# A top-6 expert layer on one core: routed rows scattered plainly to a place per token, weighted and summed at the end

## The chip, the cores and the metric

The kernel runs on one core of a Trainium2 chip. The metric is the device time of one execution in microseconds. The core has five engines that run their own instruction streams and meet at semaphores: PE (matmul), DVE (vector), ACT (scalar, activations), POOL (GpSimd) and SP (which only issues DMAs here). Sixteen DMA engines move data for them.

## The reference

`x` is [2, 512, 256], so T = 1024 tokens of H = 256. `xn = layernorm(x)`, and the output is `x + attention(xn) + moe(xn)`.

```
q, k, v = xn @ Wq + bq, xn @ Wk + bk, xn @ Wv + bv        # 8 heads of 32
# decayed linear attention, head h with factor g[h], per sequence of 512:
out[i] = sum over j <= i of g**(i-j) * (q[i].k[j]) * v[j]   # done in chunks, with a carried state

scores = softmax(xn @ gate_w.T)                            # 64 experts
topk_w, topk_ids = top_k(scores, 6);  topk_w /= sum(topk_w) + 1e-20
routed = sum over the 6 experts e of a token:
           topk_w * (silu(xn @ Wg[e]) * (xn @ Wu[e])) @ Wd[e]   # inner width 176
shared = (silu(xn @ SG) * (xn @ SU)) @ SD                  # inner width 352
moe = routed + shared
```

## The kernel before, in words

The kernel is written engine by engine; each engine's block is its program in order, and every dependency is a semaphore wait.

**Routing.** `x` is loaded as 8 chunks of 128 tokens, normalised on DVE into `tab`, and written by POOL to the HBM tensor `table` (1024 rows: 256 values of the token and 64 weights, one per expert, zero where the expert wasn't chosen). PE makes the logits, DVE finds the top six (`chosen`), PE counts ranks, and one-hot matmuls turn them into lists of up to 128 tokens per expert, a column of `gidx` each (gather indices; padding points beyond the table and is skipped) and of `sidx` (scatter indices; padding points to spare rows behind the 1024). POOL computes the normalised weights. Q, K and V are made on PE in the same stage. POOL also zeroes two accumulators `acc[0]` and `acc[1]` of 1152 rows in HBM.

**Experts.** 66 tiles follow: one for each of 64 experts and two extra ones (`EXTRA`) for experts with more than 128 tokens (a loop behind them for still more isn't entered with these inputs). Tile t, with k its place in a ring of 16: SP loads the weights (480 and 48 KB) into a slot of the ring up to 16 tiles ahead. POOL gathers the tile's rows (`gather`, L423) 8 tiles ahead with the index column `gcol`. PE transposes them (L1090), ACT and DVE split them and the weights in a high and a low part (L547, L775; L541 and `w_low`, L770), PE multiplies (L1104, six matmuls), ACT applies silu (L553), DVE multiplies gate, up and the token's weight (`gate_up`, L762), PE transposes (L1114) and multiplies by the down weights (L1132, L1133), ACT copies the result from PSUM to `y` (`evac_y`, L566; four buffers), and POOL adds the 128 rows to `acc[k % 2]` (`scatter`, L429, an indirect DMA that accumulates). Two scatters into one accumulator must not be under way together, so `store` waits for the one two tiles earlier:

```
pool.wait_ge(acc_done[k % 2], (t - k) * 8 + 16 * (k // 2 + 1))
pool.sem_inc(pool_waited, 1)
scatter(k)
```

POOL's order is: gather for tile t + 8, scatter of tile t - 1, and so on. DVE writes the columns `scol` (L858) and `gcol` (L863) at the end of each tile's work. The lists of the two extra tiles are made during the last tiles; their gathers come `LATE` = 4 places later than the rhythm, directly ahead of the scatters of tiles 59 and 60.

**Shared expert and attention.** PE multiplies six blocks (L1202) with DVE's product (`sprod`, L940, in the buffer of `y`, so the first one waits for all scatters) and ACT's silu; between them DVE adds biases to K and V, scales K (`ks`) and Q (`qsT`) and copies `kT`. Then 8 chunks of 128 tokens: scores on PE (`scores`, L1213), the product by `decay` on DVE (L968), the shared expert's down matmuls (L1236), the state's matmul and its update on DVE (L987; L991 and L992 from the second chunk of a sequence on; none in the fourth), the output matmuls (L1256) into the same PSUM bank, and DVE's final addition into `res` (L978, L997), which SP stores. What it adds was loaded from the two accumulators (1 MB each) and summed with `x_again` by POOL, 16 additions (L499, L502).

## Time and profile before

| | |
|---|---|
| time, median of 3 runs | 343.68 us (342.89 to 348.36) |
| profiled execution, its own time | 344.82 us |
| its span, first to last instruction | 343.0 us |
| mean granted TensorE clock | 0.943 of full speed |
| PE / DVE / ACT / POOL busy | 297.7 / 189.1 / 152.0 / 225.6 us |
| DMA moved | 64.88 MB |
| first expert matmul (L1104) | 50.57 us |
| last expert matmul (L1133) ends | 279.9 us |

Busy time is the union of an engine's instructions; waits and semaphore handling aren't in it. The difference between the profiled execution's time and its span, 1.8 us, lies before the first and behind the last instruction.

### The profile page before, as it was taken

Reading aid. Unit: us, or ns where it says so; the run is one execution under the profiler, and the core shown is the slowest. Engines: PE = TensorE matmul, PEld = TensorE weight load, DVE = VectorE, ACT = ScalarE, POOL = GpSimd, SP = SyncE. Lnnn points to the kernel's source line nnn. Section 1 sums busy time; section 2 is a strip of 40 time slices with the busy share of each in tenths; the row PEclk is TensorE's granted clock in tenths of the full one; section 3 lists DMA queues with packets and bytes.
Section 4 is the critical chain, followed back from the end, with each engine's and each line's share of the span. In section 5 each row is a group of like instructions: output and inputs, shape, how many; then the busy total and the mean of one; then the engine's idle time right before and its main releaser. Section 6 shows DMA issues by size and latency. Waiting matters only on the chain.

```text
span 343.0 us, 6367 instructions
## 1 busy us (share of the span) xinstructions
PE 297.7 (87%) x1608; PEld 211.0 (62%) x1608; DVE 189.1 (55%) x541; ACT 152.0 (44%) x400; POOL 225.6 (66%) x176
## 2 busy tenths in 40 slices
PE   8938888998798778979798988899883999989996
PEld 7814766775476655646465665677562643549996
DVE  4587758863544444535455454548762245845553
ACT  1635356665554646455555556465661232230000
POOL 1566547877787778878888788888865555359200
PEclk9996999999879899999999999969998589999999
DMA  7999619999989798999889999877962436300000
GB/s 204 361 396 341 188 43 309 274 268 264 247 209 241 174 286 210 232 245 235 235 228 241 239 223 256 234 160 174 208 122 35 46 35 145 129 0 32 32 32 32
DMA packets 34870, 64.88 MB, mean 189 GB/s; under 512 B 5451, under 2 KB 23063, under 8 KB 34848
## 3 DMA queue, kind: packets, MB, share of 16 engines
q1 hardware_dynamic: 21216, 44.42, 41.0%
q0 software_dynamic: 13632, 20.20, 29.7%
q8 instruction: 10, 0.16, 0.2%
q14 instruction: 12, 0.10, 0.1%
HBM read 54.17 MB, written 13.37 MB: 197 GB/s over the span
## 4 chain that ended last, share of the span: by engine, by line
DMA 31%; PE 28%; issue 17%; DVE 10%; POOL 10%; ACT 2%; POOLq 1%; SPq 0%; DVEq 0%; ACTq 0%
DMA acc<-y,scol 28%; PE ps L1104 6%; POOL acc L429 6%; POOL digits L423 4%; PE ps L1256 3%; PE ps L1202 3%; PE ps L1133 3%; PE ps L1236 2%; PE ps L1132 2%; DVE one_hots L715 2%; PE ps L1213 2%; DMA digits<-table,gcol 2%; PE ps L1090 1%; DMA x_slab<-in_x 1%; DVE neg_max L694 1%
## 5 line engine op out<-in xcount | busy, mean ns | idle before, releaser
L429 POOL DMA_INDIRECT acc<-y,scol x66 | 105.7, 1602 | 36.0 <-issue 16.7
L1104 PE MATMUL ps<-w_split,xT_both 128*128 128x352 f32 x396 | 92.6, 362 | 25.0 <-ACT xT_both L547 24.4
L1104 PEld LDWEIGHTS ps<-w_split,xT_both 128*128 128x128 f32 x396 | 64.8, 198 | 57.9 <-ACT w_split L541 30.1
L423 POOL DMA_INDIRECT digits<-table,gcol x66 | 76.4, 1158 | 23.4 <-issue 15.2
L762 DVE SCALAR_TENSOR_TENSOR act<-ps,digits,sg 128x176 f32<-128x176 f32 x64 | 25.6, 400 | 93.0 <-ACT sg L553 91.0
L566 ACT COPY y<-ps 128x256 f32<-128x256 f32 x66 | 24.7, 374 | 94.4 <-DMA acc<-y,scol 78.8
L770 DVE TENSOR_TENSOR w_split<-w_ring,w_split 128x704 fp32r<-128x704 f32 x66 | 58.3, 884 | 1.1 <-PE ps L1104 0.3
L541 ACT CAST w_split<-w_ring 128x704 fp32r<-128x704 f32 x66 | 51.7, 784 | 0.0
L1133 PE MATMUL ps<-w_slab,aT 48*128 48x256 f32 x132 | 48.5, 449 | 0.0
L1132 PE MATMUL ps<-w_ring,aT 128*128 128x256 f32 x132 | 43.2, 412 | 0.0
L1133 PEld LDWEIGHTS ps<-w_slab,aT 48*128 48x128 f32 x132 | 20.6, 196 | 24.2 <-issue 24.2
L1090 PE MATMUL ps<-k,digits 128*128 128x128 f32 x132 | 26.8, 286 | 6.6 <-DMA digits<-table,gcol 6.6
L775 DVE TENSOR_TENSOR xT_both<-ps,xT_both 128x256 fp32r<-128x256 f32 x66 | 27.4, 415 | 6.9 <-ACT xT_both L547 6.8
L1114 PE MATMUL ps<-k,act 128*128 128x128 f32 x132 | 27.2, 291 | 0.0
L547 ACT CAST xT_both<-ps 128x256 fp32r<-128x256 f32 x66 | 24.6, 373 | 5.6 <-PE ps L1090 5.3
L559 ACT COPY aT<-ps 128x256 f32<-128x256 f32 x66 | 25.6, 388 | 0.4
L553 ACT ACTIVATE sg<-ps 128x176 f32<-128x176 f32 x66 | 21.1, 320 | 8.8 <-PE ps L1104 7.8
L1090 PEld LDWEIGHTS ps<-k,digits 128*128 128x128 f32 x132 | 19.2, 147 | 8.9 <-DMA digits<-table,gcol 6.1
L1132 PEld LDWEIGHTS ps<-w_ring,aT 128*128 128x128 f32 x132 | 21.9, 208 | 0.3 <-issue 0.3
L1202 PE MATMUL ps<-xnT,sgu_sb 128*128 128x512 f32 (+1 forms) x48 | 21.4, 595 | 0.6 <-ACT y L566 0.6
L1114 PEld LDWEIGHTS ps<-k,act 128*128 128x128 f32 x132 | 17.9, 150 | 0.5 <-issue 0.5
L491 POOL TENSOR_TENSOR sact_lo<-y,sact_hi 128x512 fp32r<-128x512 f32 (+1 forms) x6 | 8.4, 1412 | 12.4 <-ACT sact_hi L631 12.4
(161 smaller groups left out, 356.1 us busy)
## 6 DMA issues: line engine op xcount, KB each, us to landing
w_ring<-in_w SPq DMA_DIRECT2D x66, 480.0 KB, 3.7
w_slab<-in_w SPq DMA_DIRECT2D x66, 48.0 KB, 4.4
acc<-zero POOLq DMA_DIRECT2D x2, 1152.0 KB, 16.5
routed_sums<-acc SPq DMA_DIRECT2D x2, 1024.0 KB, 7.0
digits<-table,gcol POOLq DMA_INDIRECT x66, 4.2
acc<-y,scol POOLq DMA_INDIRECT x66, 5.2
x_slab<-in_x SPq DMA_DIRECT2D x4, 256.0 KB, 3.4
table<-tab_slab POOLq DMA_DIRECT2D x1, 1024.0 KB, 9.1
```

Source lines behind the costliest of these rows:

```text
L423: pool.indirect_dma_start(out=rows[:, r, :], out_offset=None, in_=table, in_offset=bass.IndirectOffsetOnAxis(ap=gcol[:, r:r + 1], axis=0), ...
L429: pool.indirect_dma_start(out=acc[k % 2], out_offset=bass.IndirectOffsetOnAxis(ap=scol[:, k % 8:k % 8 + 1], axis=0), in_=y[:, k % 4, :], i ...
L541: nc.scalar.copy(rr(w_hi[:, k % 4, :]), w1_sb[:, k % RING, 0:4 * F]).then_inc(whi_sb, 1)
L559: nc.scalar.copy(aT[:, k % 2, :], ps[4 + k % 2][:, 0:2 * P]).then_inc(aT_sb, 1)
L770: V.tensor_tensor(rr(w_lo[:, k % 2, :]), w1_sb[:, k % RING, 0:4 * F], w_hi[:, k % 4, :], ALU.subtract).then_inc(wlo_sb, 1)
L775: V.tensor_tensor(rr(xT_lo[:, k % 2, :]), ps[k % 2][:, 0:H], xT[:, k % 2, :], ALU.subtract)\
L1090: ins = nc.tensor.transpose(ps[k % 2][:, h * P:(h + 1) * P], rows[:, r, h * P:(h + 1) * P], ident)
L1104: ins = mm(ps[2 + k % 2][:, 0:2 * F], rr(a[:, k % 2, h * P:(h + 1) * P]), rr(b[:, k % (2 if b is w_lo else 4), h * 2 * F:(h + 1) * 2 * F]) ...
L1114: ins = nc.tensor.transpose(ps[4 + k % 2][:, h * P:(h + 1) * P], act[:, k % 2, h * P:(h + 1) * P], ident)
L1132: mm(ps[6 + k % 2][:, 0:H], aT[:, k % 2, 0:P], w1_sb[:, slot, 4 * F:W1C], start=True, stop=False)
L1133: mm(ps[6 + k % 2][:, 0:H], aT[0:F2, k % 2, P:2 * P], w2_sb[0:F2, slot, :], start=False, stop=True).then_inc(y_ps, 1)
L1202: ins = mm(ps[(m % 2) * 2 + o][0:fw, :], sgu_sb[:, k, o * FS + f * P:o * FS + f * P + fw], xnT[:, k, n * 512:(n + 1) * 512], start=(k == 0 ...
```

## The change

Nothing is accumulated in HBM any more. Each token gets six rows of a new HBM tensor `parts` (6144 rows of 256), one for each expert it chose. The row's number for token and expert is found by a running count over `chosen` (`dest`), and it takes the place of the weight in the table's last 64 columns, so that it comes with the gathered row. `scol` is made from it; padding points beyond `parts` and is skipped. DVE's product in `gate_up` no longer has the token's weight. `store` waits only for `y` and `scol`; the four buffers of `y` have a semaphore each (`y_out`), for which ACT's copy waits four tiles later. After the experts SP loads `parts` chunk by chunk ([128, 6, 256], three buffers), ACT scales each of the six rows by its weight (`part_w`, which DVE makes in the shared expert's stage with six pairs of a product and a reduction over the 512 columns), and DVE reduces the six to one and adds `x_again`, into which it has put the PSUM result. POOL's 16 additions, the zeroing and the two loads of 1 MB go.

```diff
-    acc = [nc.dram_tensor(f"acc{k}", [ACC_ROWS, H], f32, kind="Internal").ap() for k in range(2)]
+    parts = nc.dram_tensor("parts", [T * TOPK, H], f32, kind="Internal").ap()
...
-            for k in range(2):
-                sp.dma_start(acc_sb[k], acc_v[k][:, 0:NC, :]).then_inc(acc_in, 16)
-            for c in range(NC):
-                sp.wait_ge(res_sb, c + 1)
-                sp.dma_start(out_v[:, c, :], res[:, c % 2, :]).then_inc(out_done[c % 2], 16)
+            for c in range(NC + PART_BUFS):
+                if c >= PART_BUFS:
+                    done = c - PART_BUFS
+                    sp.wait_ge(res_sb, done + 1)
+                    sp.dma_start(out_v[:, done, :], res[:, done % 2, :]).then_inc(out_done[done % 2], 16)
+                if c < NC:
+                    if c >= PART_BUFS:
+                        sp.wait_ge(parts_read, c - PART_BUFS + 1)
+                    b = c % PART_BUFS
+                    sp.dma_start(part_sb[b], parts_v[:, c, :, :]).then_inc(parts_in[b], 16)
...
-            for k in range(2):
-                pool.dma_start(acc_v[k], zero[:].unsqueeze(1).to_broadcast([P, ACC_ROWS // P, H]))\
-                    .then_inc(acc_done[k], 16)
...
+            pool.wait_ge(dest_ready, 1)
+            pool.dma_start(table_v[:, :, H:ROW], dest.rearrange("p (c e) -> p c e", e=E)).then_inc(table_out, 16)
             pool.wait_ge(share_ready, 1)
...
             def scatter(k):
                 pool.indirect_dma_start(
-                    out=acc[k % 2], out_offset=bass.IndirectOffsetOnAxis(ap=scol[:, k % 8:k % 8 + 1], axis=0),
-                    in_=y[:, k % 4, :], in_offset=None, compute_op=ALU.add).then_inc(acc_done[k % 2], 16)
+                    out=parts, out_offset=bass.IndirectOffsetOnAxis(ap=scol[:, k % 8:k % 8 + 1], axis=0),
+                    in_=y[:, k % Y_BUFS, :], in_offset=None, bounds_check=T * TOPK - 1,
+                    oob_is_err=False).then_inc(y_out[k % Y_BUFS], 16)
...
                 pool.wait_ge(scol_ready, t + 1)
-
-                pool.wait_ge(acc_done[k % 2], (t - k) * 8 + 16 * (k // 2 + 1))
                 pool.sem_inc(pool_waited, 1)
                 scatter(k)
...
-            for c in range(NC):
-                G.tensor_tensor(acc_sb[1][:, c, :], acc_sb[1][:, c, :], acc_sb[0][:, c, :], ALU.add)\
-                    .then_inc(pool_step, 1)
-                pool.wait_ge(pool_step, c + 1)
-                G.tensor_tensor(acc_sb[1][:, c, :], acc_sb[1][:, c, :], x_again[:, c, :], ALU.add)\
-                    .then_inc(xab_ready, 1)
...
-                    act_e.wait_ge(acc_done[k % 2], (t - k) * 8 + 16 * (k // 2))
-                nc.scalar.copy(y[:, k % 4, :], ps[6 + k % 2][:, 0:H]).then_inc(y_sb, 1)
+                    act_e.wait_ge(y_out[k % Y_BUFS], (t - k) * (16 // Y_BUFS) + 16 * (k // Y_BUFS))
+                nc.scalar.copy(y[:, k % Y_BUFS, :], ps[6 + k % 2][:, 0:H]).then_inc(y_sb, 1)
...
             high_product(5)
+            act_e.wait_ge(part_w_ready, TOPK)
+            for c in range(NC):
+                act_e.wait_ge(parts_in[c % PART_BUFS], 16 * (c // PART_BUFS + 1))
+                for k in range(TOPK):
+                    ins = nc.scalar.activation(part_sb[c % PART_BUFS][:, k, :], part_sb[c % PART_BUFS][:, k, :],
+                                               ACT.Identity, scale=part_w[:, c, k:k + 1])
+                ins.then_inc(parts_scaled, 1)
...
             dve.wait_ge(chosen_ready, 1)
+            dve.wait_ge(ex_ready, NC)
+            dve.wait_ge(c32_in, 16)
+            flat = chosen[:].rearrange("p c e -> p (c e)")
+            V.tensor_tensor_scan(dest[:], flat, flat, c_32("dest_first"), ALU.add, ALU.max).then_inc(dest_ready, 1)
...
-                V.tensor_copy(scol[:, k % 8:k % 8 + 1], sidx[:, bass.ds(t, 1)]).then_inc(scol_ready, 1)
+                    V.scalar_tensor_tensor(scol[:, k % 8:k % 8 + 1], rows[:, k % AHEAD, bass.ds(t + H, 1)], -1.0,
+                                           pad[:, bass.ds(t, 1)], ALU.add, ALU.add).then_inc(scol_ready, 1)
...
+            def part_weights(k):
+
+                if k > 0:
+                    dve.wait_ge(part_w_ready, k)
+                V.scalar_tensor_tensor(ov_sel[:], dest.rearrange("p (c e) -> p c e", e=E), float(k), exm[:],
+                                       ALU.is_equal, ALU.mult).then_inc(dve_step, 1)
+                step[0] += 1
+                dve.wait_ge(dve_step, step[0])
+                V.tensor_reduce(part_w[:, :, k], ov_sel[:], AX, ALU.add).then_inc(part_w_ready, 1)
...
+                if n == 0:
+                    dve.wait_ge(comb_ready, 1)
+                    V.tensor_tensor(dest.rearrange("p (c e) -> p c e", e=E), dest.rearrange("p (c e) -> p c e", e=E),
+                                    bc(c_32("dest_base"), [P, NC, E]), ALU.subtract).then_inc(rel_ready, 1)
+                    dve.wait_ge(rel_ready, 1)
+                part_weights(n)
...
+            def finish(c):
+                dve.wait_ge(o_ps, 2 * (c + 1))
+                if c == 0:
+                    dve.wait_ge(x_again_in, 32)
+                V.tensor_tensor(x_again[:, c, :], ps[4 + c % 2][:, 0:H], x_again[:, c, :], ALU.add)\
+                    .then_inc(o_sb, 1)
+
+            def sum_parts(c):
+                dve.wait_ge(parts_scaled, c + 1)
+                V.tensor_reduce(total[:, c % 2, :],
+                                part_sb[c % PART_BUFS].rearrange("p k h -> p h k"), AX, ALU.add).then_inc(parts_read, 1)
+                dve.wait_ge(parts_read, c + 1)
+                dve.wait_ge(o_sb, c + 1)
+                if c >= 2:
+                    dve.wait_ge(out_done[c % 2], 16 * (c // 2))
+                V.tensor_tensor(res[:, c % 2, :], x_again[:, c, :], total[:, c % 2, :], ALU.add).then_inc(res_sb, 1)
...
                 if c >= 1:
-                    finish = c - 1
-                    dve.wait_ge(xab_ready, finish + 1)
...
+                    finish(c - 1)
                 m = c % SEQ_CHUNKS
                 if m == SEQ_CHUNKS - 1:
+                    sum_parts(c - 1)
                     continue
...
+                if c >= 1:
+                    sum_parts(c - 1)
+            finish(NC - 1)
+            sum_parts(NC - 1)
```

The extra tiles get their destinations from the gathered rows too, with two small operations each (`extra_dest`) that were made for the weight before.

## Rows read from the trace of the kernel before

**Rows 1.** The page's chain that ended last, by engine and line.

```profile
DMA acc<-y,scol 28%; PE ps L1104 6%; POOL acc L429 6%; POOL digits L423 4%; PE ps L1256 3%; PE ps L1202 3%; PE ps L1133 3%; PE ps L1236 2%; PE ps L1132 2%; DVE one_hots L715 2%; PE ps L1213 2%; DMA digits<-table,gcol 2%; PE ps L1090 1%; DMA x_slab<-in_x 1%; DVE neg_max L694 1%
```

**Rows 2.** Waits from 66 to 270 us: total, times, longest.

```profile
ACT y L566 <- DMA acc<-y,scol: 78.8, 46, 4.3
```

**Rows 3.** The page's DMA issues; the last number is us to landing.

```profile
acc<-y,scol POOLq DMA_INDIRECT x66, 5.2
```

**Rows 4.** Scatters and gathers, 66 to 250 us: ns shortest/median/longest, first and last start.

```profile
L429 POOL DMA_INDIRECT acc<-y,scol x53: 1578/1582/2188, 68.1 to 248.5; - x53
L423 POOL DMA_INDIRECT digits<-table,gcol x53: 1046/1052/1725, 66.1 to 246.5; - x53
```

**Rows 5.** Timeline of POOL, 120 to 172 us: start, duration, idle before.

```profile
140.26 1.58 POOL L429 DMA_INDIRECT acc<-y,scol  x1 [0.30 <-issue]
...
143.51 1.58 POOL L429 DMA_INDIRECT acc<-y,scol  x1 [0.31 <-issue]
```

**Rows 6.** Windows: length, PE, PEld, DVE, ACT, POOL busy, clock, DMA share, GB/s.

```profile
130.00:150.00 20.00, 17.19 (x86) 11.75 (x84) 9.91 (x30) 10.21 (x29) 16.32 (x12) 1.00 0.90 230
```

**Rows 7.** Timeline, 54 to 61 us.

```profile
54.72 1.30 PE L1104 MATMUL ps<-w_split,xT_both 128*128 128x352 f32 x6 [0.33 <-ACT xT_both L547]
...
57.45 1.35 PE L1104 MATMUL ps<-w_split,xT_both 128*128 128x352 f32 x6
...
58.81 0.89 DVE L770 TENSOR_TENSOR w_split<-w_ring,w_split 128x704 fp32r<-128x704 f32 x1
...
58.86 1.72 POOL L423 DMA_INDIRECT digits<-table,gcol  x1 [0.30 <-issue]
```

**Rows 8.** The chain that ended last, in order of time: start, us.

```profile
50.57 1.29 PE ps L1104 x6
```

**Rows 9.** Timeline of PE, 256 to 284 us.

```profile
264.86 0.69 PE L1090 MATMUL ps<-k,digits 128*128 128x128 f32 x2 [5.78 <-DMA digits<-table,gcol]
...
267.91 2.13 PE L1104 MATMUL ps<-w_split,xT_both 128*128 128x352 f32 x6
...
272.83 2.13 PE L1104 MATMUL ps<-w_split,xT_both 128*128 128x352 f32 x6
```

**Rows 10.** Windows behind that stall.

```profile
266.00:268.00 2.00, 2.00 (x5) 0.70 (x4) 1.28 (x3) 0.37 (x1) 1.70 (x2) 0.50 0.49 59
```

**Rows 11.** Windows, the shared expert's stage.

```profile
287.00:305.00 18.00, 16.44 (x50) 7.14 (x48) 14.06 (x22) 6.53 (x13) 6.14 (x5) 1.00 0.39 117
```

**Rows 12.** DVE: a scan (by tile) and the wait for ranks (timeline).

```profile
L751 DVE TENSOR_TENSOR_SCAN ov<-ov_ones,ov x1: 344/344/344, 46.5 to 46.5; 128x64 f32<-128x64 f32 x1
...
27.37 0.69 DVE L705 SCALAR_TENSOR_TENSOR rank_i<-chosen,ps 128x512 int32<-128x512 f16 x1 [2.34 <-PE ps L1043]
```

**Rows 13.** Groups, 50 to 287 us: total busy us, mean ns of one.

```profile
L541 ACT CAST w_split<-w_ring 128x704 fp32r<-128x704 f32 x64 | 50.2, 784 | 0.0
...
L806 DVE TENSOR_REDUCE ov_rank<-route 128x8 f32<-128x512 f32 x2 | 1.3, 674 | 0.0
...
L786 DVE TENSOR_REDUCE ov_s<-ov 128x1 f32<-128x64 f32 x2 | 0.4, 220 | 0.1
```

**Rows 14.** Timeline, the end of the experts and the first product behind it.

```profile
279.18 0.70 PE L1133 MATMUL ps<-w_slab,aT 48*128 48x256 f32 x2
...
286.75 0.69 DVE L940 TENSOR_TENSOR y<-ps,w_slab 128x512 f32<-128x512 f32 x1 [4.34 <-DMA acc<-y,scol]
```

**Rows 15.** Timeline, 305 to 343 us: a chunk of the attention and the end.

```profile
305.85 1.29 DVE L968 TENSOR_TENSOR pT<-ps,k 128x512 f32<-128x512 f32 x2 [0.93 <-PE ps L1213]
...
315.95 0.73 PE L1213 MATMUL ps<-x_slab,kT 32*128 32x128 f32 x16
...
317.13 0.29 DVE L991 TENSOR_TENSOR route<-ps,k 128x128 f32<-128x128 f32 x1 [1.42 <-PE ps L1245]
...
318.61 1.28 DVE L968 TENSOR_TENSOR pT<-ps,k 128x512 f32<-128x512 f32 x2
...
340.37 0.42 DVE L997 TENSOR_TENSOR res<-ps,routed_sums 128x256 f32<-128x256 f32 x1 [2.74 <-issue]
```

137 lines of the change are left out of this document (68 added, 69 removed).

## The prediction

> **What bounds the kernel now.** I read the chain of work that ended last first: its largest entry by far is the transfer of the accumulating scatter, 28% of the span [rows 1]. The waits of the expert stage say who feels it: the copy of an expert's result out of PSUM waits 78.8 us in total for such a transfer [rows 2]. One scatter takes 5.2 us from issue to landing [rows 3], and a scatter may start only when the one two tiles earlier has landed, so this chain alone allows a tile per 2.6 us plus issue and waits, about 3.2. But POOL stands right beside it: a scatter and a gather are 1.58 and 1.05 us [rows 4], each with 0.30 us of issue in front, which makes 3.23 us, and that is the very distance of two scatters in a quiet stretch [rows 5]. Windows show POOL busy 16.3 of 20 us there and 12 of its DMA instructions, so 6 tiles per 20 us, 3.33 each; the DMA share is 0.90 [rows 6]. PE is the third candidate: before scatters matter, two tiles start 2.73 us apart at full clock [rows 7]. So the expert stage, from 50.6 [rows 8] to 279.9 us (229.3 us, 66 tiles, 3.47 each), is held by the scatters' landing and by POOL's instructions, with PE 0.7 us per tile behind.
>
> Two disturbances lie on top. Near the end PE stands still for 5.8 us until the gather of the first extra tile lands [rows 9]; in POOL's order that gather is behind a scatter, whose source waited for an older scatter. After it the granted clock reads 0.50, the 1.2 GHz level [rows 10], and a tile takes 4.92 us (267.91 to 272.83) [rows 9].
>
> From 279.9 on the bound changes: PE and DVE share the rest. DVE is busy 14.1 of 18 us in the shared expert's stage [rows 11].
>
> **The expert stage.** Removed: the wait of each scatter for the one two before, the read of the destination, and the rows of the padding (66 x 128 = 8448 rows, of which 1024 x 6 = 6144 are real, so 2304). The wait for a free `y` buffer stays, but it now looks four tiles back at a plain write. With a landing of 5.2 us, kept from the slower kind, plus 2 us of issue and copy, four buffers allow a tile per 1.8 us: this limit is gone. What is late next is POOL. The new scatter's duration is in no row. Bounds: 1.05 us, the gather's, which also moves 128 listed rows with a bounds check, and 1.58 us, the accumulating one's, which has no bounds check [rows 4]. Below 1.0 I see no reason to go, as the list of rows stays. I take the gather's end, because what the change strips is just the difference between the two kinds: per row a second read, which fits their ratio of 1.5. POOL's pair is then 2 x (1.05 + 0.30) = 2.70 us.
>
> To that comes a collision. A gather that begins inside DVE's `w_low` subtraction is longer: the one at 58.86 us took 1.72 us where the subtraction ran from 58.81 to 59.70 [rows 7], and the median is 1.05 [rows 4]. The subtraction is 0.89 us of a tile of about 2.9, so a start falls into it with chance 0.3 and then loses about 0.45 us on average; two starts a tile make 0.25 us. POOL's pair becomes 2.95 us, over PE's 2.73. The stage: 50.6 + 66 x 2.95 = 245.3 instead of 279.9, a gain of 34.6 us. In it is the stall of 5.8 us with its slow stretch: the extra tile's gather no longer stands behind a wait for a landing, and POOL has four tiles without a gather just before it, 4 x 1.35 us to catch up.
>
> The Trainium skill speaks to that collision: "SBUF — State Buffer", section "Who interferes with whom", says that a DVE instruction with two SBUF inputs contends with a GpSimd instruction that reads SBUF, but infers that a tensor_tensor leaves descriptor generation alone. The 1.72 us row disagrees with the inference; by the page the pair would stay 2.70, PE's 2.73 would set the pace, and the result would be the faster rival's below.
>
> DMA: 0.90 of 3.33 us is 3.0 us of transfer time per tile. A quarter fewer scatter rows, without their read, must save at least 0.3 of it, so 2.7 us against a pace of 2.95; weights run 14 experts ahead, so I cost it at nothing; if that cover goes the pace rises, which is inside the range. On ACT and DVE the edits are even: the weighted product loses its scalar, `scol` comes from an addition in place of a copy. DVE's `scol` reads the gathered row one tile later than the old weight was read, and the gather into that row is queued behind `gcol`, which was written after `scol` already.
>
> **Before the stage.** DVE gets a scan of 512 elements. A scan of 64 took 0.34 us, so it costs between 0.34 and 2.8 us; DVE idled 2.34 us at this place for the ranks on PE [rows 12]. From 64 elements to 512 I expect near 1 us: nothing. Its further wait for ACT's exponentials ends about when it starts. Behind it is the rank step, so the cost without cover would be 0.5 us. Fewer index operations give back 0.3 us. The table's second part moves past POOL's weight product and goes out earlier; the two zeroing transfers vanish, off the chain. Net -0.3 us.
>
> **The shared expert's stage.** It got no slack on DVE. Added there: one subtraction of 512 elements and six pairs of a product (0.69 us [rows 12]) and a reduction (0.67 us [rows 13]). With links a pair is 1.45 us and all come to 9.5 us, on an engine that was busy for 14.1 of 18. What is gained: DVE's first product waited for the last accumulating scatter until 286.75, which is 6.85 us after PE's last expert matmul at 279.9 [rows 14]; now the last plain scatter should land about 5 us after it. Following DVE's order: the subtraction and two pairs stand ahead of the last bias, for which PE waits before its transposes, and later pairs before each next product. Stepwise that puts the first product by `decay` 29.3 us behind the last expert matmul, against 25.95 (305.85 minus 279.9) [rows 14, 15]: +3.4 us.
>
> **The attention stage.** Removed from POOL: 16 additions, hidden. Added on ACT: 48 scalings of 256 columns; 704 columns take 0.78 us [rows 13], so each is under 0.4 and six are under 2.4 us per chunk, below the chunk's period: hidden. The eight loads of 768 KB read three ahead from SP's queue: hidden too, and they delay the stores of the output only by their issue. Added on DVE per chunk: a reduction of 1536 elements and an addition. Reductions took 0.22 us for 64 and 0.67 for 512 [rows 13], a slope of 1.0 ns, which gives 1.7 us; by plain proportion to the larger it would be 2.0. With the addition at 0.4 and links, 2.15 us. DVE and PE take turns here: scores on PE, product by `decay` on DVE, next scores. From the start of scores to the first state operation are 1.18 us (315.95 to 317.13), from there to the next product 1.48 (317.13 to 318.61), the product is 1.29 [rows 15]. With the sum in this loop it closes in 1.18 + 1.48 + 2.15 + 1.29 + 0.05 = 6.15 us where it took 4.6: +1.55 us in each of the four chunks with two-step states. The chunk with short states adds 0.7, the two without states 0.9 together, and behind the last chunk's matmuls the reduction and the addition are bare: 2.15. Sum +10 us.
>
> **The sum.** The profiled execution took 344.8 us, 343.0 of span and 1.8 around it. 344.8 - 34.6 - 0.3 + 3.4 + 10.0 = 323.3. That execution was 1.1 us above the median of the runs shown, 343.7, so the forecast is 322 us. 2% (about what a measurement tells from no change) is 337 and 351.
>
> **Rivals.** (1) The plain scatter costs POOL what the accumulating one does. For it: the bounds check is new and the list is as long; against it: the gather with its check is 1.05. The pair is 3.23 + 0.13 (the mean excess now) = 3.36, the stage ends at 272.4, and the time is 344.8 - 7.5 + 13.1 = 350 us, slower. It decides from a scatter of 1.5 us on; beyond 1.6 the loss passes 2%. (2) PE's clock falls in the last stage. PE was busy 19.8 of 20 us there, and it would stand idle a third of each 6.15 us. Speaking for it: it fell where PE stood still for 5.8 us [rows 9, 10]; against it, it held at 1.00 where PE was busy 17.2 of 20 [rows 6]. At the lower level a chunk's 4.3 us (34.5 us for eight, 305.85 to 340.37) [rows 15] becomes 7.7, 1.5 more than the loop: +10 us, 333. The skill's page "TensorE: Matmul & The Clock Gate", section "What's actually happening", says that recent activity sets the clock, which fits these rows. (3) No collisions, PE sets the pace at 2.75, and the sums on DVE fall partly into idle: stage end 232.1, +10 behind it: 344.8 - 47.8 - 0.3 + 10 = 306.7 us. (4) The accumulation was never what bound and the new waits on `y_out` replace it: the landing would have to stay above 10 us, which no row supports; 344 us.
>
> **How the numbers follow.** Chances: forecast 0.56, rival 1 0.09, rival 2 0.15, rival 3 0.15, rival 4 0.05. The range from 306 to 338 takes in rivals 2 and 3 and the unknown width of POOL's pair (2.75 to 3.2). Faster by over 2%: 0.56 + 0.15 + 0.15 less what of the slow side of these passes 337, 0.84. Rivals 1 and 4 end mostly within 2%: 0.10 with the rest; slower 0.06.
>
> **What would show it.** The scatter's mean duration near 1.05, or 1.58 in rival 1. Its waits gone from the copy of `y`, POOL's idle almost all issue, scatters 2.9 to 3.0 us apart. No stall of PE near the extra tiles. DVE busy nearly throughout after the experts, PE waiting for the product by `decay` in each chunk, chunks 6 us apart, and 2 us between the last attention matmul and the last store. I am wrong if POOL's pair stays above 3.2 us, if transfers become the wait of ACT's weight copy, or if the granted clock falls in the attention stage.

## The result and the profile after

The changed kernel takes 359.98 us (median of 4 runs, 357.93 to 362.08), the kernel before 343.28 us beside it (342.04 to 348.36): a ratio of 1.050, with an interval of 1.042 to 1.058. It is slower by 5%, where 322 us was forecast. Executions of one kernel differ by some per cent, the longer ones with a lower granted clock, so each ratio goes by the faster executions alone, and the tables name the time of the one that was profiled.

Two lengths split the profiled executions, and they are used for every run below. The *stage* is the time from the first gate and up product to the end of the last expert matmul; the *tail* is the rest of the span behind it. A *pause* is a stretch of the stage of over 0.6 us in which TensorE's rows show no matmul.

| | before | after | predicted |
|---|---|---|---|
| last expert matmul ends at | 279.9 | 267.6 | 245.0 |
| stage, us (66 tiles) | 229.3 | 218.4 | 194.7 |
| tail, us | 63.1 | 91.0 | 76.5 |
| profiled execution, us | 344.8 | 360.3 | 323.3 |

So of the 37.0 us that separate the sum from the measurement, 22.6 have come up by the end of the stage (23.7 in it, less 1.1 from an earlier start) and 14.4 lie in the tail. Against the kernel before, the start comes 1.4 us earlier, the stage is 10.9 us shorter and the tail 27.9 us longer: the kernel is slower because of its tail, and misses the forecast gain above all in its stage.

The first thing to read is what the change was made for. The page's groups of the changed kernel (total busy us, mean ns | idle before, what ended most of it):

```profile
L439 POOL DMA_INDIRECT digits<-table,gcol x66 | 71.7, 1086 | 62.1 <-DVE gcol L882 23.6
...
L445 POOL DMA_INDIRECT parts<-y,scol x66 | 71.9, 1089 | 25.8 <-issue 21.4
...
L574 ACT COPY y<-ps 128x256 f32<-128x256 f32 x66 | 24.8, 375 | 48.6 <-PE ps L1179 40.5
```

The scatter takes 1.09 us on average (1.02 in the median) where the median was 1.58 [rows 4], and the copy of `y` waits for TensorE and no longer for a transfer [rows 2]. GpSimd now stands idle for 62 us ahead of its gathers, 23.6 of them for VectorE's `gcol`. It doesn't bound any more, and yet a tile takes 3.31 us on average. The timeline shows where the time goes (start, duration, idle before):

```profile
184.91 0.70 PE L1179 MATMUL ps<-w_slab,aT 48*128 48x256 f32 x2
185.08 0.37 ACT L574 COPY y<-ps 128x256 f32<-128x256 f32 x1 [2.55 <-remote]
185.35 0.78 ACT L549 CAST w_split<-w_ring 128x704 fp32r<-128x704 f32 x1
186.36 1.01 POOL L445 DMA_INDIRECT parts<-y,scol  x1 [0.60 <-issue]
187.27 0.32 ACT L561 ACTIVATE sg<-ps 128x176 f32<-128x176 f32 x1 [1.14 <-remote]
187.62 0.34 DVE L779 TENSOR_TENSOR act<-ps,sg 128x176 f32<-128x176 f32 x1 [4.08 <-ACT sg L561]
...
188.52 1.42 PE L1150 MATMUL ps<-w_split,xT_both 128*128 128x352 f32 x6 [2.91 <-ACT xT_both L555]
...
189.73 0.63 PE L1136 MATMUL ps<-k,digits 128*128 128x128 f32 x2
```

The `Silu` at 187.27 needs the gate product that TensorE had started at 182.87 and that takes 1.24 us, so it could have begun behind the cast at 186.13. It waits 1.14 us more, and the page can't say for whom ("remote" is a releaser that it doesn't know). TensorE's signal came some 3 us after the end that its own row gives; the ends of matmul rows are modelled, so the rows can't tell whether the product or only its signal was late. ScalarE, VectorE and TensorE wait in turn for this one, TensorE for 2.91 us, while GpSimd works on. Behind it the clock is down: two transposes take 0.63 us in place of 0.38. Between such places the tiles start 2.66 us apart. The changed kernel has 13 pauses, 21.1 us in sum, the five longest of 1.67 to 3.00 us, from 83 to 217 us. The kernel before had 17, 24.0 us in sum with the one of 5.78 [rows 9]; the others were at most 2.7 us, and I hadn't read them as a pattern. Windows of 40 us (length, busy us of PE, PEld, DVE, ACT, POOL, then clock, DMA share, GB/s):

```profile
60.00:100.00 40.00, 36.17 (x166) 26.07 (x165) 21.30 (x70) 22.75 (x59) 23.98 (x23) 0.87 0.69 225
100.00:140.00 40.00, 35.23 (x160) 25.94 (x160) 18.91 (x56) 22.55 (x57) 23.53 (x24) 0.87 0.66 218
140.00:180.00 40.00, 35.30 (x178) 25.77 (x176) 20.62 (x65) 24.27 (x64) 25.43 (x25) 0.96 0.73 232
180.00:220.00 40.00, 33.47 (x159) 24.31 (x158) 18.41 (x57) 22.23 (x57) 24.61 (x24) 0.91 0.69 221
```

Where the clock was at 1.00 in a quiet stretch before [rows 6], it is now 0.87 to 0.96, and the DMA engines are less busy (0.66 to 0.73 against 0.90), so they aren't what is short.

The tail, as groups of VectorE from 268 us to the end, and as windows:

```profile
L1005 DVE TENSOR_REDUCE aT<-token_rows 128x256 f32<-128x1536 f32 x6 | 16.8, 2793 | 0.0
L1020 DVE TENSOR_TENSOR pT<-ps,k 128x512 f32<-128x512 f32 x16 | 10.2, 682 | 0.0
...
L1011 DVE TENSOR_TENSOR res<-tab_slab,aT 128x256 f32<-128x256 f32 x8 | 3.4, 425 | 0.3
```

```profile
268.00:290.00 22.00, 19.44 (x57) 8.95 (x57) 19.23 (x30) 6.00 (x12) 8.98 (x7) 1.00 0.29 109
290.00:310.00 20.00, 16.99 (x110) 13.56 (x111) 12.28 (x22) 10.02 (x23) 4.22 (x3) 0.74 0.00 1
310.00:330.00 20.00, 18.03 (x158) 16.98 (x156) 17.80 (x22) 5.45 (x14) 0.00 (x0) 0.83 0.43 138
330.00:358.50 28.50, 20.85 (x120) 19.95 (x118) 20.91 (x28) 7.07 (x18) 0.00 (x0) 0.55 0.25 79
```

The reduction takes 2.79 us, not 1.7, eight times (six of them in the group shown), and VectorE goes into those six without idling: it is in line with the product by `decay`. Two such products, with a reduction between them:

```profile
312.78 1.28 DVE L1020 TENSOR_TENSOR pT<-ps,k 128x512 f32<-128x512 f32 x2
...
316.67 2.80 DVE L1005 TENSOR_REDUCE aT<-token_rows 128x256 f32<-128x1536 f32 x1
...
319.85 1.28 DVE L1020 TENSOR_TENSOR pT<-ps,k 128x512 f32<-128x512 f32 x2
```

The clock falls to 0.55 at the end. It is down once before any reduction has run (the first starts at 309.58):

```profile
294.00:300.00 6.00, 3.38 (x42) 2.86 (x43) 4.52 (x6) 3.97 (x10) 2.96 (x2) 0.89 0.01 1
300.00:308.00 8.00, 8.00 (x48) 7.55 (x48) 2.20 (x5) 4.68 (x12) 0.00 (x0) 0.50 0.01 2
```

### The profile page after: what moved, and what is told of

It reads as the page before. It is cut to its first block, busy times and chain, and to the rows that moved or that the text cites. A ratio compares the mean times of both kernels' runs of the same rounds, so it can differ in the third digit from the quotient of the medians.

```text
span 358.5 us, 6350 instructions
## 1 busy us (share of the span) xinstructions
PE 311.3 (87%) x1608; PEld 230.7 (64%) x1608; DVE 220.6 (62%) x565; ACT 178.1 (50%) x448; POOL 175.3 (49%) x158
## 4 chain that ended last, share of the span: by engine, by line
PE 67%; DVE 17%; issue 5%; another core or an unknown queue 3%; DMA 3%; ACT 3%; POOL 1%; SPq 0%; DVEq 0%; POOLq 0%; ACTq 0%
PE ps L1150 21%; PE ps L1179 13%; PE ps L1178 8%; PE ps L1302 5%; PE ps L1136 5%; PE ps L1160 4%; PE ps L1282 3%; DVE aT L1005 2%; PE ps L1259 2%; DVE one_hots L734 2%; DMA digits<-table,gcol 2%; DVE route L945 1%; PE ps L1291 1%; PE ps L1297 1%
## 5 line engine op out<-in xcount | busy, mean ns | idle before, releaser
L1150 PE MATMUL ps<-w_split,xT_both 128*128 128x352 f32 x396 | 87.8, 360 | 21.7 <-ACT xT_both L555 14.5
L439 POOL DMA_INDIRECT digits<-table,gcol x66 | 71.7, 1086 | 62.1 <-DVE gcol L882 23.6
L1150 PEld LDWEIGHTS ps<-w_split,xT_both 128*128 128x128 f32 x396 | 66.0, 200 | 47.3 <-issue 45.6
L445 POOL DMA_INDIRECT parts<-y,scol x66 | 71.9, 1089 | 25.8 <-issue 21.4
L779 DVE TENSOR_TENSOR act<-ps,sg 128x176 f32<-128x176 f32 x66 | 22.5, 341 | 85.2 <-ACT sg L561 60.7
L1178 PE MATMUL ps<-w_ring,aT 128*128 128x256 f32 x132 | 44.5, 423 | 0.0
L561 ACT ACTIVATE sg<-ps 128x176 f32<-128x176 f32 x66 | 21.0, 318 | 32.1 <-remote 13.7
L1136 PE MATMUL ps<-k,digits 128*128 128x128 f32 x132 | 27.6, 294 | 2.0 <-DMA digits<-table,gcol 1.3
L660 ACT ACTIVATE token_rows<-token_rows,part_w 128x256 f32<-128x256 f32 x36 | 14.9, 495 | 28.1 <-DMA token_rows<-parts 26.3
L1302 PEld LDWEIGHTS ps<-kv,pT 128*128 128x128 f32 x128 | 23.7, 278 | 0.0
L1302 PE MATMUL ps<-kv,pT 128*128 128x32 f32 x128 | 23.1, 340 | 0.0
```

The lines of the kernel that those rows point to most:

```text
L439: pool.indirect_dma_start(out=rows[:, r, :], out_offset=None, in_=table, in_offset=bass.IndirectOffsetOnAxis(ap=gcol[:, r:r + 1], axis=0), ...
L445: pool.indirect_dma_start(out=parts, out_offset=bass.IndirectOffsetOnAxis(ap=scol[:, k % 8:k % 8 + 1], axis=0), in_=y[:, k % Y_BUFS, :], i ...
L1136: ins = nc.tensor.transpose(ps[k % 2][:, h * P:(h + 1) * P], rows[:, r, h * P:(h + 1) * P], ident)
L1150: ins = mm(ps[2 + k % 2][:, 0:2 * F], rr(a[:, k % 2, h * P:(h + 1) * P]), rr(b[:, k % (2 if b is w_lo else 4), h * 2 * F:(h + 1) * 2 * F]) ...
L1178: mm(ps[6 + k % 2][:, 0:H], aT[:, k % 2, 0:P], w1_sb[:, slot, 4 * F:W1C], start=True, stop=False)
L1302: ins = mm(bank[:, at:at + D], pT[:, u % 4, h * P:(h + 1) * P], kv[:, c, H + at:H + at + D], start=False, stop=(h == HG - 1 and g == 1))
```

## The experiments

Eighteen kernels were run. Those called "without the end's sums" are compared among themselves. "us" is the median of a kernel's executions, "profiled" the time of the one from which the columns behind it are read, "indirect" the number of indirect DMAs under way at some time between 60 and 220 us, "clock" the mean granted clock there.

| kernel | us | profiled | stage | tail | pauses: number, us | indirect | clock |
|---|---|---|---|---|---|---|---|
| before | 343.3 | 344.8 | 229.3 | 63.1 | 17, 24.0 | 93 | 0.97 |
| after | 360.0 | 360.3 | 218.4 | 91.0 | 13, 21.1 | 93 | 0.90 |
| e2 scatter waits two back | 356.9 | 355.5 | 215.8 | 91.8 | 14, 24.4 | 97 | 0.93 |
| e3 sums on GpSimd | 340.4 | 343.8 | 218.9 | 74.9 | 14, 23.5 | 94 | 0.89 |
| e4 light weights | 361.6 | 357.6 | 215.8 | 93.6 | 13, 29.5 | 95 | 0.95 |
| e5 GpSimd + 0.43 us | 349.3 | 346.1 | 205.4 | 92.5 | 12, 16.3 | 101 | 0.95 |
| e6 GpSimd + 0.68 us | 369.6 | 365.2 | 220.2 | 95.6 | 17, 22.6 | 94 | 0.97 |
| e7 half-width products | 384.7 | 383.2 | 244.4 | 90.9 | 15, 20.5 | 85 | 0.92 |
| e17 tree of additions | 350.3 | 341.9 | 213.4 | 79.4 | 19, 26.6 | 98 | 0.97 |
| e16 e3 and e5 together | 332.5 | 328.4 | 206.9 | 71.4 | 13, 16.6 | 99 | 0.95 |
| *without the end's sums:* | | | | | | | |
| e1 nothing else | 329.3 | 323.1 | 212.1 | 63.0 | 17, 22.2 | 98 | 0.94 |
| e8 stores on SyncE | 291.2 | 291.4 | 179.9 | 63.0 | 2, 1.7 | 56 | 1.00 |
| e9 plain stores on GpSimd | 293.3 | 293.1 | 179.9 | 63.0 | 2, 1.8 | 56 | 1.00 |
| e14 e9 with a busy GpSimd | 295.5 | 299.3 | 186.5 | 63.0 | 1, 2.9 | 54 | 0.97 |
| e10 accumulating, no wait | 331.5 | 330.6 | 219.5 | 63.0 | 19, 24.3 | 96 | 0.98 |
| e11 all 128 rows | 332.1 | 333.9 | 218.2 | 67.6 | 15, 24.1 | 94 | 0.92 |
| e12 rows of 256 bytes | 332.1 | 333.9 | 222.9 | 63.0 | 15, 27.2 | 94 | 0.90 |
| e13 64 rows | 330.8 | 330.7 | 217.9 | 63.0 | 19, 25.0 | 94 | 0.91 |
| e15 e8 with two gathers | 339.7 | 343.3 | 230.6 | 63.0 | 18, 31.7 | 92 | 0.89 |
| e18 two in every other tile | 305.3 | 307.9 | 195.3 | 63.0 | 4, 6.4 | 84 | 0.96 |

### The end

**e1, without the sums.** Weights per token, loads, scalings and reductions are gone; `finish` writes `res` itself.

```
-                ins.then_inc(parts_scaled, 1)
...
-                V.tensor_tensor(x_again[:, c, :], ps[4 + c % 2][:, 0:H], x_again[:, c, :], ALU.add)
+                V.tensor_tensor(res[:, c % 2, :], ps[4 + c % 2][:, 0:H], x_again[:, c, :], ALU.add)
```

> The changed kernel without its end's sums: no weights per token, no loads of the six rows, no scaling on ScalarE, no sum on VectorE; the experts' contribution is left out of the output, which holds x, attention and the shared expert. The profile of the changed kernel gives 90.9 us from the last expert matmul to the end, 63.1 before. Theory A (the sums cost the tail its +27.8 us and nothing else): the tail goes back to 61 to 65 us, the expert stage stays at 3.3 us a tile with its pauses, the time is 360 - 28 = about 332 us. Rival B (half of the tail is TensorE at its lower clock, which the pauses of the expert stage bring on, not the sums): the tail stays above 75 us, time 345 or more.

Theory A holds: the tail is 63.0 us, that of the kernel before (63.1). Windows of its tail:

```profile
280.00:300.00 20.00, 18.37 (x193) 15.78 (x192) 10.49 (x24) 1.81 (x4) 3.47 (x3) 1.00 0.06 21
300.00:321.20 21.20, 18.60 (x191) 17.72 (x189) 9.57 (x23) 0.00 (x0) 0.00 (x0) 1.00 0.10 32
```

With the sums gone the clock stays at 1.00 too, although the stage has its 17 pauses as ever, so these don't bring the clock's fall in the tail.

**e3, the sums on GpSimd.**

```
+            for c in range(NC):
+                pool.wait_ge(parts_scaled, c + 1)
+                pb = part_sb[c % PART_BUFS]
+                padd(pb[:, 0:3, :], pb[:, 3:6, :])
+                padd(pb[:, 0, :], pb[:, 1, :])
+                padd(pb[:, 0, :], pb[:, 2, :])
+                padd(x_again[:, c, :], pb[:, 0, :])
```

> The changed kernel with the six scaled rows and x summed on GpSimd (four adds a chunk of 768, 256, 256 and 256 columns) in place of VectorE's reduction, whose one instruction takes 2.83 us; VectorE has the one last add a chunk, as before. Theory A (the reduction on VectorE paces the end: 6.2 to 7.6 us a chunk against 4.6 before): the tail falls from 90.9 to 65 to 72 us, time 335 to 342. Rival B (GpSimd takes over as the bound, or its port stretches VectorE's own work): the tail stays at 80 us or above, time 350 or more.

The tail falls to 74.9 us, outside Theory A's 65 to 72 and far under Rival B's 80, and the time to 340.4 us, inside A's range: a ratio to the kernel before of 0.983 (0.977 to 0.989), a gain of less than 2%. Taking the sums off VectorE gives back 16.1 of the tail's 27.9 us. The clock still falls in it for a while (0.57 and 0.56 between the second and the fourth product by `decay`). The groups of GpSimd in its tail:

```profile
L519 POOL TENSOR_TENSOR token_rows<-token_rows 128x256 f32<-128x256 f32 (+1 forms) x18 | 19.6, 1091 | 5.2 <-ACT token_rows L676 3.7
...
L519 POOL TENSOR_TENSOR tab_slab<-tab_slab,token_rows 128x256 f32<-128x256 f32 x6 | 4.4, 726 | 0.5
```

Three additions of 1.09 us on average and one of 0.73 are 4.0 us a chunk on an engine that has nothing else to do there.

**e17, a tree of additions on VectorE.** Same engine, same place, another way to sum.

```
-                V.tensor_reduce(total[:, c % 2, :], part_sb[...].rearrange("p k h -> p h k"), AX, ALU.add)
+                link(V.tensor_tensor(pb[:, 0:3, :], pb[:, 0:3, :], pb[:, 3:6, :], ALU.add))
+                link(V.tensor_tensor(pb[:, 0, :], pb[:, 0, :], pb[:, 1, :], ALU.add))
+                V.tensor_tensor(total[:, c % 2, :], pb[:, 0, :], pb[:, 2, :], ALU.add)
```

> The changed kernel with VectorE's one reduction of 1536 columns a chunk (2.79 us; it reads the six rows 256 columns apart) as three additions of 768, 256 and 256 columns that read along the rows, about 1.0 + 0.42 + 0.42 us by the changed kernel's own rows of 512 and 256 columns, and two small waits between them. Theory P (the prediction's sum for the end was right but for the size of this one instruction, 1.7 us in it): the tail falls from 90.9 to 76 to 83 us, time 345 to 353. Rival Q (the end is long for another reason: TensorE's lower clock, or the chain through ScalarE's scaling): the tail stays at 88 us or more, time 357 or more.

```profile
L1006 DVE TENSOR_TENSOR token_rows<-token_rows 128x768 f32<-128x768 f32 x6 | 5.7, 950 | 0.0
...
L1007 DVE TENSOR_TENSOR token_rows<-token_rows 128x256 f32<-128x256 f32 x6 | 2.6, 425 | 0.2
L1008 DVE TENSOR_TENSOR aT<-token_rows 128x256 f32<-128x256 f32 x6 | 2.6, 425 | 0.2
```

The sum costs 0.95 + 0.43 + 0.43 = 1.80 us a chunk in place of 2.79, about what the prediction had assumed for it, and the tail is 79.4 us, about what it had forecast (76.5). Theory P's numbers are there, but its cause only in part. The profiled execution is the shortest of four (341.9 to 357.1 us), and its clock didn't fall ahead of the first sum, where the changed kernel's did, though TensorE's busy time is the same there (3.33 of 6 us against 3.38, then the stretch behind it):

```profile
287.00:293.00 6.00, 3.33 (x47) 2.91 (x48) 4.73 (x7) 3.96 (x10) 2.96 (x2) 1.00 0.00 1
293.00:301.00 8.00, 7.49 (x75) 7.02 (x73) 5.70 (x14) 4.75 (x12) 0.00 (x0) 1.00 0.01 2
```

The first three products by `decay` stand 2.95 and 7.35 us apart here, 3.91 and 11.60 in the changed kernel. That is 5.2 of the 11.5 us between the two tails, and the one sum in this stretch accounts for only 1.0 of it. The ratio to the kernel before is 1.021 (0.997 to 1.045), which is unclear.

### The pauses of the stage

**e2, waiting two back,** as the accumulating scatter had to.

```
+                if k >= 2:
+                    pool.wait_ge(y_out[(k - 2) % Y_BUFS], ...)
```

> The changed kernel, with each scatter of a tile waiting until the scatter of two tiles before has landed (14 of every 16 tiles), as the accumulating one had to. Theory A (the pauses of TensorE about every 4.3 tiles come from scatters that are in flight together and crowd the DMA queues): the pauses get fewer or vanish, and the expert stage goes below 215 us against 218.4, the whole below 355. Rival B (the pauses have another cause): the stage stays at 218 or gets longer by what the waits add, time 358 to 372.

Neither: 14 pauses with 24.4 us, and a stage 2.6 us shorter. Scatters in flight together aren't what the pauses need.

**e4, light weights.** `w1[..., 0:256]` only, in the loop.

> The changed kernel with the weight loads inside the loop over experts 17 to 64 cut to the first 256 columns of w1 (the experts' products then use stale weights in the other columns; the output is not the reference's). Theory A (the pauses of TensorE come from the weight traffic that shares the DMA engines or the memory with the scatters): the pauses vanish, a tile takes 2.7 us, the stage 180 to 190 us, time 322 to 332. Rival B (they come from the work of the engines or from the scatters alone): pauses stay every 4 tiles and the stage stays at 215 to 220, time 357 to 362.

Rival B. From 60 to 220 us the DMA share falls from 0.69 to 0.41, and 8 of the 13 pauses are 2.19 us or longer, the last five of them (166.8 to 221.5 us) 13.7 us apart, in every fourth tile. It isn't the traffic of the weights.

**e5 and e6, a slower GpSimd.**

```
                 scatter(k)
+                pool.wait_ge(slack_done, t + 1)
+                G.tensor_tensor(slack[:, 0:64], zero[:, 0:64], zero[:, 0:64], ALU.add).then_inc(slack_done, 1)
```

> The changed kernel with one short addition (128x64, into a buffer that nothing reads) on GpSimd after each scatter of a tile, so that GpSimd sets a pace between 2.7 and 3.1 us a tile. The undisturbed tile of the changed kernel takes 2.66 us, yet TensorE pauses for up to 3.0 us about every 4.3 tiles and the mean is 3.31. Theory R (the pauses are the price of TensorE's own pace: at a slower steady pace they vanish): pauses over 2 us are gone, the mean tile is 3.0 to 3.15, the stage 198 to 210 us against 218, time 340 to 352. Rival S (the pauses come from something that happens once in 4 tiles whatever the pace): they stay, the stage is 218 to 235 us, time 360 to 375.

> As the run before it, with an addition of 128x256 (0.73 us on GpSimd by the trace): pace about 3.4 us a tile. Theory R: no pauses over 1 us, a stage of 66 x 3.4 = 225 to 232 us, as the kernel before has, with a granted clock near 1 through it; time 360 to 370. Rival S: the pauses stand on top, the stage is 240 us or more, time 380 or more.

e5 is as Theory R has it in time (349.3 us, stage 205.4), though pauses of up to 2.15 us stay: with *more* work on GpSimd the kernel is 11 us faster (no execution of the one, 345.7 to 354.9 us, overlaps those of the other; they weren't run side by side, and the kernel before took 344.8 and 343.3 us beside them). e6's time, 369.6, is in Theory R's range, but its stage, 220.2, is under R's and it has pauses of 2.4 to 2.7 us (3.3 at the extra tiles), which R forbids; Rival S's 240 isn't there either. Both theories were too simple.

**e7, more TensorE instructions.** Each product of 352 columns as two of 176.

> The changed kernel with each of the six gate and up products of a tile (352 columns) as two of 176 columns: 12 more instructions a tile on TensorE (6 products and 6 weight loads, 40 in place of 28), the same columns. Theory R1 (the pauses come after a number of TensorE instructions, whose records and semaphore updates come late): they come every 3 tiles in place of 4.3, the mean tile is 3.6 us or more, the stage 235 us or more, time 375 or more. Rival R2 (they come after so much work or time of the array, or have nothing to do with TensorE): they stay about 4.3 tiles apart, the stage is 218 to 225 us, time 360 to 367.

The time and the stage (244.4 us) are those of R1, the pattern isn't: an undisturbed tile takes 2.98 us (2.66 in the changed kernel), and the larger pauses stand 4 or 5 tiles apart, not 3. It isn't the number of TensorE's instructions.

**e8, the stores on SyncE's queue,** so that GpSimd only gathers:

```
-                    store(i * RING + (k - 1), k - 1)
...
+                sp.wait_ge(y_sb, i * RING + (s + 1))
+                sp.dma_start(direct[s * P:(s + 1) * P, :], y[:, s % Y_BUFS, :])
```

> The run without the end's sums (329.3 us, stage 212 us), whose scatters on GpSimd are taken away too: each tile's rows go to a fixed place in DRAM by a plain DMA on SyncE's queue, and GpSimd only gathers; the output holds x, attention and the shared expert. Theory G (the pauses come from GpSimd's indirect scatters, two indirect DMAs a tile filling something up about every 8.5): they vanish or come half as often, the stage falls to 185 to 200 us, time 303 to 317. Rival T (they come from TensorE's pace): they stay, the stage is 205 to 220 us, time 322 to 337.

Theory G, beyond its own numbers (185 to 200 us and 303 to 317 us): 291.2 us, with a stage of 179.9. The pauses over 1 us are gone, TensorE works without a break and at full clock:

```profile
100.00:140.00 40.00, 40.00 (x212) 29.73 (x211) 24.75 (x76) 28.91 (x76) 15.30 (x15) 1.00 0.95 297
140.00:180.00 40.00, 40.00 (x212) 29.70 (x210) 24.65 (x76) 28.90 (x77) 15.22 (x15) 1.00 0.94 301
```

**e9, plain stores on GpSimd.** `pool.dma_start(direct[...], y[...])` in place of the indirect one.

> The run without the end's sums, with each tile's rows stored by a plain DMA to a fixed place that GpSimd issues in place of the indirect one (the output holds x, attention and the shared expert). The scatters' absence has just taken the pauses away: stage 179.9 us against 212.1. Theory I (it is the indirect scatter, its list of 128 places, that brings the pauses on): they vanish, the stage is 178 to 190 us, time 290 to 302. Rival J (it is any second DMA a tile that GpSimd makes up in software): they stay, the stage is 205 to 216 us, time 320 to 333.

Theory I, with e8's stage of 179.9 us to the tenth. Timeline of GpSimd:

```profile
175.17 1.04 POOL L433 DMA_INDIRECT digits<-table,gcol  x1 [1.04 <-ACT y L566]
176.21 0.59 POOL L440 DMA_DIRECT2D direct<-y  x1
```

A second software DMA a tile is harmless if it isn't indirect. It is also shorter, so GpSimd is less busy, and that had to be told apart:

**e14, e9 with a busy GpSimd** (an addition of 128x256 a tile).

> The run with the plain stores issued by GpSimd (stage 179.9 us, no pauses, GpSimd at work for 1.04 + 0.59 us a tile), with an addition of 128x256 (0.68 us) on GpSimd a tile, which brings its work to 2.4 us and more of the 2.66 us of a tile (the output holds x, attention and the shared expert). Theory X (indirect DMAs themselves, two a tile, bring the pauses on): none comes back, the stage is 178 to 186 us, time 291 to 299. Rival Y (GpSimd at work nearly without a break does): they come back, the stage is over 200 us, time over 313.

```profile
L435 POOL DMA_INDIRECT digits<-table,gcol x54 | 58.3, 1080 | 15.1 <-issue 7.9 <-DVE gcol L872 4.1 <-ACT y L571 3.1
L460 POOL TENSOR_TENSOR slack<-zero 128x256 f32<-128x256 f32 x58 | 47.1, 812 | 1.2
L442 POOL DMA_DIRECT2D direct<-y x59 | 34.9, 591 | 3.7 <-ACT y L571 2.1 <-issue 0.8 <-DVE scol L866 0.8
```

From 60 to 220 us GpSimd is at work for 140 of 160 us and TensorE doesn't pause once. The stage, 186.5 us, is 6.6 us longer than e9's, behind one pause of 2.9 us at 53.4, early in the stage, and half a microsecond over Theory X's range; the profiled execution took 299.3 us, the other one 291.6, for e9's 293.3. Theory X; a busy GpSimd alone doesn't bring the pauses on.

**e10 to e13, four kinds of scatter,** on the kernel without sums: accumulating (`compute_op=ALU.add`); 128 regular places, none skipped; rows of 64 columns; 64 rows.

> The run without the end's sums, with the scatter accumulating again as in the kernel before, but to a place of its own per token and with no wait for the one before (the output holds x, attention and the shared expert). Theory K (plain scatters bring the pauses on, accumulating ones do not): no pauses over 2 us; GpSimd paces the tile at 1.05 + 1.6 + 0.6 = 3.25 us, the stage is 210 to 220 us with the clock near 1. Rival L (the kernel before escaped the pauses by its waits or its pace alone, and the kind of write does not matter): the pauses stay on top of the slower pace, the stage is 225 us or more.

> The run without the end's sums, with each scatter writing all 128 rows of its tile to 128 places that only depend on the tile's number, none skipped by the bounds check, and places 48 rows apart (the output holds x, attention and the shared expert). Theory M (rows that are skipped, or places that are spread unevenly, bring the pauses on): they vanish, stage 178 to 190 us, time 290 to 302. Rival N (neither matters, two indirect DMAs a tile do): they stay, every 4 tiles, stage 208 to 220 us, time 322 to 335.

> The run without the end's sums, with each scattered row cut to its first 64 columns (256 bytes in place of 1024) in an array of its own: a quarter of the bytes, the same number of rows and descriptors (the output holds x, attention and the shared expert). Theory B (the bytes written to scattered places in DRAM bring the pauses on): they vanish or shrink to a quarter, stage 180 to 190 us. Rival D (the number of descriptors or of indirect DMAs does): the stage stays at 208 to 216 us, time 322 to 333.

> The run without the end's sums, with each scatter writing only the first 64 rows of its tile: still two indirect DMAs a tile, with 192 rows in place of 256 (the output holds x, attention and the shared expert). Theory D (it is the number of rows or descriptors a second that brings the pauses on): they thin out by a quarter or vanish, and the stage falls to 180 to 200 us from 212 to 219. Rival W (it is the number of indirect DMAs, or GpSimd at work without a break): if one takes as long as before, they stay, the stage is 208 to 222 us; if GpSimd's 1.06 us shrinks to about 0.6, the stage is 180 to 190.

None takes the pauses away: stages of 217.9 to 222.9 us. e10 is split: its stage (219.5 us) and clock (0.98) are Theory K's, its pauses (up to 3.00 us) Rival L's; accumulating scatters don't keep them away. N for e11, W for e13. e12 is D in kind and in time, with a stage of 222.9 us over D's 216. In e13 half the rows leave the scatter as long as it was (from 60 to 220 us):

```profile
L438 POOL DMA_INDIRECT parts<-y,scol x47 | 47.6, 1013 | 19.6 <-issue 16.1 <-ACT y L567 3.2 <-DVE gcol L868 0.3
```

**e15, two gathers.** e8 with a second gather a tile into a buffer that nothing reads.

```
+                extra_gather(k % AHEAD, k % 2)
                 gather(k % AHEAD)
```

> The run with the stores on SyncE's queue (stage 179.9 us, no pauses), with a second indirect gather a tile, always of the first tiles' rows, into a buffer that nothing reads (the output holds x, attention and the shared expert). So two indirect DMAs a tile again, none of them a scatter. Theory X (two indirect DMAs a tile, of either direction, bring the pauses on): they come back, every 4 tiles or so, stage 208 to 225 us, time 320 to 337. Rival Z (only scatters, that is rows written to listed places in DRAM, do): none, stage 178 to 192 us, time 290 to 305.

Theory X in kind, beyond its numbers (stage 230.6 us for 208 to 225; 343.3 us in the profiled execution, 336.2 in the other): 18 pauses with 31.7 us come back into a kernel that had 2. So the scatter isn't needed for them. Two windows beside e8's:

```profile
100.00:140.00 40.00, 35.90 (x157) 26.29 (x156) 19.11 (x58) 22.19 (x58) 23.91 (x24) 0.84 0.84 261
140.00:180.00 40.00, 33.83 (x151) 25.16 (x151) 17.60 (x55) 20.91 (x53) 21.60 (x22) 0.85 0.83 260
```

**e18, the second gather in every other tile.**

> The run with two gathers a tile (stage 230.6 us), with the second gather in every other tile only: three indirect DMAs in two tiles (the output holds x, attention and the shared expert). At the undisturbed pace of 2.7 us a tile that is one indirect DMA every 1.8 us. All runs with two a tile and no slower engine made 92 to 98 of them in the 160 us from 60 to 220, one every 1.63 to 1.74 us, whatever their kind; those with one a tile made about 60. Theory V (GpSimd's indirect DMAs can't be sustained faster than about one every 1.65 us, and the pauses are how the excess is paid): at one every 1.8 us no pause over 2 us, the stage is 180 to 190 us. Rival U (every second indirect DMA of a tile brings its share of pauses, whatever the rate): half of the pauses are there, the stage is 196 to 210 us.

Its windows:

```profile
60.00:100.00 40.00, 35.65 (x160) 26.03 (x159) 19.61 (x61) 21.82 (x57) 20.82 (x20) 0.83 0.82 253
100.00:140.00 40.00, 38.69 (x202) 28.13 (x200) 23.52 (x71) 26.80 (x72) 23.47 (x22) 1.00 0.94 296
140.00:180.00 40.00, 38.70 (x202) 28.34 (x201) 24.59 (x74) 27.54 (x73) 22.83 (x21) 1.00 0.94 298
```

The stage, 195.3 us, ends between the two. Three of its four pauses (1.47 us at 53.2, 2.82 at 67.0 and 1.36 at 74.0) fall before 75 us, with a low clock behind them; from there to the end of the stage there is one, of 0.7 us. That is Theory V's picture with a rough start, not half of the pauses all along. The other execution took 302.7 us, 5.2 less than the profiled one, so its stage may have been about 190 us, an estimate that puts the whole difference there.

Against a simple limit on the rate stands e7. Between its pauses it asks for an indirect DMA every 1.49 us (two in 2.98 us). By Theory V the pauses would bring that back to about 1.65. It gets 85 in the 160 us, one every 1.88 us, no more often than e18 with its 84, and has 15 pauses with 20.5 us all the same. Whether it is a rate over a shorter stretch, or the second indirect DMA in *every* tile, stays open.

**e16, what helped, together.** e3 and e5 in one kernel, which computes the reference.

> A version that computes the reference and joins two edits: the six rows and x summed on GpSimd at the end (340.4 us by itself) and a short addition after each scatter, which slows GpSimd to about 3.0 us a tile (349.3 us in place of 360 by itself). Theory (the two gains add, 20 and 11 us, since one is in the end and one in the expert stage): 326 to 334 us, so 3 to 5% under the kernel before. Rival (the added instruction gave its gain by chance of the clock's state at the end, or the last stage pays it back): 338 to 345 us.

332.5 us (328.4 to 339.5), a ratio to the kernel before of 0.967 (0.959 to 0.974). That is inside the theory's 326 to 334 us: 27.5 us under the changed kernel, for 31 if the two gains added in full.

## Why the prediction was wrong

**What bounds the kernel: wrong, and this is the step that failed.** "So the expert stage ... is held by the scatters' landing and by POOL's instructions, with PE 0.7 us per tile behind." And then: "What is late next is POOL", with a pair of 2.95 us a tile. Both named bounds were taken away, and the stage lost 10.9 of its 229.3 us in place of the 34.6 forecast. GpSimd isn't late next either: it idles 62.1 us ahead of its gathers (the sign of "idle almost all issue" isn't there), and between the pauses the tiles start 2.66 us apart, closer than its forecast pair. What holds the stage at 3.31 us a tile is stops of the whole pipeline that no group and no wait of the page names, with a lower clock behind many of them, and the kernel before had them too (17, 24.0 us).

Shown: it takes two indirect DMAs a tile; with the gather alone, the stage is 179.9 us (e8, e9), and a second gather brings the stops back (e15). No run has the scatter alone. A scatter isn't needed (e15), nor a busy GpSimd (e14 has one and no stops), and none of these takes them away: fewer bytes (e12), fewer rows (e13), no skipped rows (e11), accumulation (e10), waits (e2), lighter weights (e4). Not shown: that a rate is the limit. The kernels with two a tile have 92 to 101 of them in 160 us (85 in e7), but in them that number is only twice the number of tiles, so it says no more than the length of the stage does. For a rate speak e18 and e5, where a slower GpSimd helps; against it speaks e7. Open: why TensorE's signals are what comes late.

**The scatter's duration: right.** 1.09 us mean, with 1.05 taken. Rival 1 falls. The collision is real and was over-priced: the 11 gathers of the changed kernel that start inside the `w_low` subtraction take 1.35 us on average, the other 55 take 1.03; for the scatters it is 1.27 (15) and 1.04 (51). That is a fifth of the starts and not 0.3, and it makes 0.13 us a tile and not 0.25. The Trainium skill, page "SBUF — State Buffer", section "Who interferes with whom", says that TensorE and ScalarE never wait on anyone at the memory's ports. No run here looks at the ports by themselves; what e15 against e8 shows is that TensorE and ScalarE do stand still when GpSimd makes two indirect DMAs a tile, by whatever way.

**The stall at the extra tiles: right.** It is gone; the last pause is at 216.6 us, and tiles 64 and 65 run through.

**DMA hidden, no landing wait: right,** and the share of 0.66 to 0.73 is below the 0.92 that was set for it (2.7 of 2.95 us). Rival 4 falls: the copy of `y` waits for no transfer. Rival 3, TensorE as the pace at 2.75 us, is the undisturbed tile (2.66), and e8's stage of 179.9 us is what it would have given.

**Before the stage:** the first product came at 49.2 us, 1.4 earlier; the other runs have it from 46.1 to 48.3, so this says nothing of 0.3 us.

**The shared expert's stage: right.** The first product by `decay` comes 29.7 us behind the last expert matmul (297.27 minus 267.55); 29.3 was forecast.

**The attention stage: the loop is right, one size is wrong.** "A slope of 1.0 ns, which gives 1.7 us" for the reduction: measured 2.79. The slope came from reductions along the row; this one reads six values 256 columns apart. The loop closes as worked out. In e17, whose sum is near the assumed size, two chunks at full clock take 6.14 and 6.15 us, for 6.15 forecast. With 2.79 + 0.43 = 3.22 us in place of 2.15 it should take 7.2, and two products by `decay` stand 7.07 us apart (312.78 to 319.85), at a mean clock of 0.71. Eight reductions that are 1.1 us longer make 8.7 us at most of the 14.4 that the tail is over its forecast; the rest goes with the clock. The scalings on ScalarE took 0.495 us for the "under 0.4", hidden all the same.

**Rival 2, the clock in the last stage: it happened,** and with it the sign of being wrong that the prediction had named, "if the granted clock falls in the attention stage": 0.50 from 300 to 308 us, then 0.83 and 0.55. The chunk that ran wholly at 0.50 took 8.50 us; without the 1.07 us by which its sum is too long that is 7.4, near the 7.7 that the rival had set. But the fall at 300 us isn't the rival's. It comes before the first sum, behind a stretch in which TensorE was busy 3.38 of 6 us while VectorE made the last of `part_w`, and the second chunk took 11.60 us for 7.35 in e17. e17 has the same busy time in that stretch and kept 1.00, so that cost can be there in one execution and missing in another, and why isn't known. How the 14.4 us divide between the reduction and the clock isn't separated further.
